# A causal attention and feed-forward block on one core: GELU by a tanh polynomial, half-tile streams, scores in batches of three, roots and squares on GpSimd

## What is computed

```python
def attention(x):                       # x: 4096 x 256
    q, k, v = split(lora_linear(x, w_attn, ...), 3)
    att = where(causal, q @ k.T / sqrt(16), -inf)
    return lora_linear(softmax(att) @ v, w_proj, ...)

def ffn(x):
    h = x
    for blk in range(3):
        y = qlora_linear(h, 2 * blk)
        y = layernorm(y, gamma[blk], beta[blk])
        y = gelu(y)                     # exact, with erf
        h = h + qlora_linear(y, 2 * blk + 1)
    return h

x = x + layernorm(attention(layernorm(x)))
x = x + layernorm(ffn(layernorm(x)))
```

## Time and profile before

| | |
|---|---|
| median of three runs | 1313.88 us |
| time of the profiled execution | 1311.47 us |
| its span, first to last instruction | 1309.7 us |
| granted TensorE clock, mean of the span | 0.990 |
| TensorE, VectorE, ScalarE, GpSimd busy in the span | 96%, 48%, 89%, 11% |
| stream, 119 to 1240 us: TensorE busy | 1105.92 of 1121 us |
| stream: ScalarE busy | 1073.11 of 1121 us |

### The profile page before, as it was taken

How to read it: one execution, slowest core, us unless ns; L and a number is a source line. 1 busy time by engine, 2 the same in 40 slices (tenths; PEclk the granted TensorE clock), 3 DMA queues, 4 the chain that set the end, 5 groups by cost and what they waited for, 6 DMA issues and landing times.

```text
span 1309.7 us, 30637 instructions
## 1 busy us (share of the span) xinstructions
PE 1257.4 (96%) x11725; PEld 534.9 (41%) x11725; DVE 629.6 (48%) x2202; ACT 1163.4 (89%) x1305; POOL 144.9 (11%) x347
## 2 busy tenths in 40 slices
PE   8998989999999999999999999999999999999956
PEld 6554434334333333333343333333333333333345
DVE  6774356334744266432743365433533355432176
ACT  4674879999999999999999999999999999999833
POOL 3321311010100000000000000000000010000043
PEclk9998989999999999999999999999999999999989
DMA  5994897786764366674754645445645474432000
GB/s 172 299 294 145 138 156 127 131 118 109 117 103 66 64 124 93 94 106 77 119 86 62 89 102 80 82 71 86 117 66 85 66 126 74 71 58 34 10 5 17
DMA packets 76498, 132.27 MB, mean 101 GB/s; under 512 B 21926, under 2 KB 37308, under 8 KB 76348
## 3 DMA queue, kind: packets, MB, share of 16 engines
q1 hardware_dynamic: 72060, 126.01, 54.5%
q10 hardware_dynamic: 4288, 4.26, 1.1%
HBM read 105.03 MB, written 20.97 MB: 96 GB/s over the span
## 4 chain that ended last, share of the span: by engine, by line
PE 74%; ACT 9%; issue 3%; DVE 2%; SPq 1%; DMA 1%; POOL 1%; ACTq 0%; DVEq 0%
PE O L1298 33%; PE S L1282 24%; PE F L205 14%; ACT probs L1224 6%; PE F L1344 2%; ACT L1224 1%; ACT L1240 1%; SPq L589 1%; ACT feed_mem L1240 1%; SPq L1129 1%; PE S L1363 1%; DMA attT<-o_div 1%; DVE tmpC L1403 0%; DMA q_op<-qk_rows 0%; DVE stC L1385 0%
## 5 line engine op out<-in xcount | busy, mean ns | idle before, releaser
L1224 ACT ACTIVATE probs<-S 128x1024 f32<-128x1024 f32 x1056 | 987.4, 1039 | 52.4 <-PE S L1282 42.1
L1298 PE MATMUL O<-probs,vg 128*32 128x512 f32 (+3 forms) x4608 | 528.6, 565 | 2.4 <-DVE o_turned L1437 1.7
L1282 PE MATMUL S<-q_op,k_op 64*128 64x512 f32 (+3 forms) x2304 | 391.5, 427 | 18.2 <-ACT probs L1224 6.5
L1282 PEld LDWEIGHTS S<-q_op,k_op 64*128 64x128 f32 x2304 | 181.9, 185 | 374.7 <-ACT probs L1224 305.3
L1205 POOL TENSOR_SCALAR_AFFINE_SELECT probs<-probs 128x512 f32<-128x512 f32 (+1 forms) x160 | 89.7, 561 | 1004.7 <-ACT probs L1224 1004.6
L1298 PEld LDWEIGHTS O<-probs,vg 128*32 128x32 f32 x4608 | 117.0, 109 | 202.1 <-issue 180.3
L1466 DVE TENSOR_TENSOR feed_mem<-F,bffn 128x512 f32<-128x512 f32 x56 | 38.7, 691 | 225.6 <-PE F L205 225.6
L205 PE MATMUL F<-wfT,feed_mem 128*32 128x256 f32 x1792 | 117.3, 384 | 0.9 <-ACT feed_mem L1240 0.9
L1472 DVE SCALAR_TENSOR_TENSOR feed_mem<-F,cols,feed_mem 128x256 f32<-128x256 f32 (+1 forms) x58 | 25.0, 473 | 138.7 <-PE F L205 138.7
L1469 DVE COPY feed_mem<-F 128x512 f32<-128x512 f32 x56 | 38.4, 686 | 81.1 <-PE F L1344 80.9
L1385 DVE BATCH_NORM_STATS2 stC<-feed_mem 128x6 f32<-128x256 f32 x172 | 64.7, 417 | 13.3 <-DVEq L1428 12.0
(11 more groups left out here) (165 smaller groups left out, 881.0 us busy)
## 6 DMA issues: line engine op xcount, KB each, us to landing
k_op<-qk_rows SPq DMA_DIRECT2D x512, 128.0 KB, 5.1
qk_rows<-parts SPq DMA_DIRECT2D x32, 512.0 KB, 4.8
q_op<-qk_rows SPq DMA_DIRECT2D x256, 64.0 KB, 5.8
k_op<-qk_rows SPq DMA_DIRECT2D x128, 64.0 KB, 2.9
x_in<-in_L_attn_x ACTq DMA_DIRECT2D x8, 512.0 KB, 5.5
feed_mem<-in_L_attn_x SPq DMA_DIRECT2D x16, 256.0 KB, 4.7
attT<-o_div SPq DMA_DIRECT2D x126, 32.0 KB, 3.6
out<-feed_mem SPq DMA_DIRECT2D x14, 256.0 KB, 2.6
```

The costliest lines, as they stand in the source:

```text
L1224: nc.scalar.activation(probs[:, n % NP, :, :], S[:, n % NS, :, :], ACT.Exp, scale=SCALE).then_inc(exp_ok, 1)
L1282: last = nc.tensor.matmul(S[:, n % NS, a, at:at + TT - q0], k_op[mine, c % RING, pair, k0:k0 + P], q_op[mine, v % QS, pair, q0:TT], start= ...
L1298: last = nc.tensor.matmul(O[h * STRIP:(h + 1) * STRIP, q0:TT], vg[:, kb, col:col + STRIP], probs[:, n % NP, a, at:at + TT - q0], start=fir ...
```

## The change

1. **GELU from tanh.** For tiles 0 to 6 the GELU is 0.5 v (1 + tanh(v p(v^2))), with a polynomial p of six degrees in the square. New parts of a half: `copy` now applies half of gamma and beta (two instructions of 128x256), `sq` squares (GpSimd), `pa`, `pb`, `pc` evaluate the polynomial (seven instructions on VectorE), ScalarE takes tanh (one instruction of 128x512 per half, in place of two for the tile) and `gate` multiplies (VectorE). Tile 7 keeps ScalarE's GELU.
2. **Roots on GpSimd.** The 84 roots of tiles 0 to 6 leave VectorE for GpSimd, as 11 instructions each.
3. **Half-tile streams.** The halves of a tile no longer follow a common order. Each keeps its own order of steps, and whichever is ready takes the bank `F`, which `plan()` locks until it is emptied. `FEED_EACH` falls from 70 to 50.
4. **Batches of three.** The planner lets three scores follow each other (`BATCH`), and weighs a switch of shape on TensorE against the time that ScalarE still has work for (`next_product`).
5. **Shared first keys.** Tiles 0 and 1 are visited in turn for each head group, from one chunk of two tiles of keys. There are 76 chunks instead of 80. Two key chunks and three query tiles are loaded early, instead of four and three. The ring of queries has four slots.

```diff
-RING, QS = 4, 3
+RING, QS = 4, 4
+EARLY_AT = {3: [("k", 0), ("q", 0)], 4: [("q", 1)], 5: [("k", 1)], 6: [("q", 2)]}
+VISITS = [(t, i) for i in range(NG) for t in range(2)] + [(t, i) for t in range(2, NT) for i in range(NG)]
...
-FEED_FROM, FEED_EACH = 24.0, 70.0
-LOW_WATER, FEED_WATER = 1, 3
+FEED_FROM, FEED_EACH = 24.0, 50.0
+BATCH, THIRD, SLACK, BACKLOG = 3, 0.25, 0.5, 10
+POOL_PARTS = ("rs", "sq")
+ROOT_POOL, SQUARE_POOL = 3.1, 1.3
...
+    if t < NT - 1 and name.startswith(POOL_PARTS):
+        return "POOL"
...
-    for m, x in enumerate(feed):
+    for x in feed:
         name, t, k, n = x
-        found = [feed[m - 1]] if m else []
+        if n:
+            found = [(name, t, k, n - 1)]
+        elif name != "project":
+            found = [(before, t, k, pieces(before, t) - 1)]
...
+    def next_product(now):
+        mine = ready["PE"]
+        score = next((x for x in mine if x[0] == "score"), None)
+        can = [x for x, at in mine.items() if at <= now and x[0] != "score"]
+        if score is not None and kind == "score" and batch < BATCH and mine[score] <= now + THIRD:
+            return score, max(now, mine[score])
...
+        def wish(x):
+            if x[0] == "weigh":
+                return 0.5 if backlog >= BACKLOG else 2
+            if due[x] <= scores / 2:
+                return 0 if kind == "feed" and x[3] else 1
+            return 4
...
+                    if t < NT - 1:
+                        a, c = tmp[:, 2, b], tmp[:, 3, b]
+                        nc.gpsimd.tensor_scalar(c, mv[:, b, 0], -1.0, None, ALU.mult)
+                        link(k, nc.gpsimd.tensor_tensor(w, r, r, ALU.mult))
+                        link(k, nc.gpsimd.tensor_tensor(w, w, v, ALU.mult))
...
+                        elif name.startswith("sq"):
+                            nc.gpsimd.tensor_tensor(u[:, rows(t, k), :], zT[:, :, toks(t, k)], zT[:, :, toks(t, k)], ALU.mult).then_inc(pool_ok[k], 1)
...
                         if t < NT - 1:
-                            for j in range(2):
-                                part_done(act, f"copy{m}", t, j)
+                            part_done(act, f"pc{m}", t, k)
+                            last = nc.scalar.activation(y[:, rows(t, k), :], y[:, rows(t, k), :], ACT.Tanh)
...
+                        if n == 5:
+                            link(k, nc.vector.tensor_scalar(y[:, b, :], u[:, b, :], GELU_POLY[6], None, ALU.mult))
+                        link(k, nc.vector.scalar_tensor_tensor(y[:, b, :], y[:, b, :], GELU_POLY[n], u[:, b, :], ALU.add, ALU.mult))
+                        nc.vector.scalar_tensor_tensor(y[:, b, :], y[:, b, :], GELU_POLY[n - 1], by, ALU.add, ALU.mult).then_inc(dve_ok[k], 1)
+                    elif name.startswith("gate"):
+                        nc.vector.scalar_tensor_tensor(zT[:, :, toks(t, k)], y[:, b, :], 1.0, zT[:, :, toks(t, k)], ALU.add, ALU.mult).then_inc(dve_ok[k], 1)
```

More of the change, by code:

```diff
@@ L965, in plan @@
             if t < NT - 1:
-                item((f"gelu{m}", t, 0), "ACT", 4.0, [(f"copy{m}", t, k) for k in range(2)], 0)
+                for k in range(2):
+                    item((f"gelu{m}", t, k), "ACT", 0.55, [(f"pc{m}", t, k)], 0)
             else:
@@ L992, in plan, with kind_of, shape_of, switch @@
             ready[engine[x]][x] = 0.0
-    scores, kind, shape = 0, None, None
+    scores, kind, shape, batch = 0, None, None, 0
+    def kind_of(x):
+        return x[0] if x[0] in ("score", "weigh") else "feed"
+    def shape_of(x):
+        return "score" if x[0] == "score" else "full" if x[0].startswith("turn") or len(x) == 4 and x[1] == NT - 1 else "strips"
+    def switch(x):
+        return 0.0 if shape_of(x) == shape else SWITCH[shape_of(x)]
+    def next_product(now):
[4 more added lines that the diff above has]
+            return score, max(now, mine[score])
+        busy = free["ACT"] + sum(us[x] for x, at in ready["ACT"].items() if at <= now + HOP)
+        first = score is not None and mine[score] <= now
+        slack = busy - (now + HOP + us[score] + SWITCH["score"]) if first else 1e9
+        pending = sum(1 for z in exp_ends[-8:] if z > now) + scores - len(exp_ends)
+        if first and pending >= NS - 1 and can:
+            slack = 1e9
+        weighed = (len([0 for x in can if x[0] == "weigh"]) and min(UNIT_OF[x[1]] for x in can if x[0] == "weigh"))
+        backlog = len(exp_ends) - weighed if weighed else 0
+        def wish(x):
[4 more added lines that the diff above has]
+            return 4
+        x = min(can, key=lambda x: (wish(x), -left.get(x, 0.0), mine[x], str(x)), default=None)
+        if first and (x is None or switch(x) + us[x] > slack + SLACK):
+            return score, now
+        return (x, now) if x is not None else (score, now)
     def landing(x):
         return LANDING_FIRST if x[0] == "moved" and x[1] < FIRST_MOVED else LANDING.get(x[0], 0.0)
+    locked, F_free, blocked = None, 0.0, {}
+    def takes_bank(x):
+        return len(x) == 4 and x[3] == 0 and (x[0] == "fold" or x[1] < NT - 1)
     exp_ends = []
```

166 lines of the change are left out of this document (106 added, 60 removed).

## The result

| | before | changed |
|---|---|---|
| median of the runs | 1313.6 us | 1305.7 us |
| smallest to largest | 1310.4 to 1315.1 us | 1303.2 to 1306.8 us |
| profiled execution, its span | 1311.5, 1309.7 us | 1305.5, 1303.7 us |
| first score to the end of the last exp, "the stream" | 1121.1 us | 1107.5 us |
| end of the last exp to the end, "the tail" | 69.6 us | 77.3 us |

The ratio is 0.9946, with an interval of 0.9935 to 0.9958, from six runs of each kernel. It is faster, by 8 us and not by the 46 forecast, and 1305.7 lies above the range. The last two rows of the table are read from the profiled executions. The stream gave 13.6 us where 48 were forecast, and the tail took 7.7 of them back where 2 were.

What follows compares the result with a forecast made beforehand. TensorE and ScalarE, both nearly full and tied by three score buffers, were taken as the bound. Terms -24 - 35 - 3 + 7 + 7 + 2 = -46 us took the profiled 1311.47 to 1265.5; predicted median 1268 us, range 1240 to 1303.

Steps and rivals of the forecast that it cites:

- Spells, -35: TensorE's order: 99 fewer rounds from scores to other work and back, at 0.35 us each, save 35 us.
- Table loads, -24: ScalarE: 42 table loads leave the stream; their 0.9% + 0.9% of the chain of waits is gained, 24 us.
- Third score +7: Score spells: a batch's third score waits for the running exp's buffer; at most 24 us, 7 taken.
- feed chain +7: Feed: late halves, with GpSimd and VectorE sharing ports, stop TensorE; 0 to 20 us, 7 taken.
- first keys -3: Loads: four fewer key chunks and a fourth query slot remove TensorE's query waits; 3 us saved (0 to 5).
- The sum of 409 us: GpSimd's busy time in the stream: cuts 90, roots 260 and squares 59 us, or 38%.
- Tail, +2 (0 to +7): After the last exp: tile 6's feed now ends at the stream's end, costing 2 us.
- C: Rival: the feed's chain leaks more and the third score costs 24 us; 1285 to 1308 us, chance 0.20.
- B: Rival: TensorE and ScalarE had waited for each other, so 20 us more go; 1236 to 1250 us, chance 0.13.
- D: Rival: slower, through GpSimd's roots held up by VectorE in each tile's chain; 1330 us, chance 0.12.
- the signs for being right: Two table loads, ScalarE about 1020 us, TensorE above 95%, stream about 1075 us, GpSimd near 410 us.
- The sign by which the forecast was to be called wrong: The stream stays over 1105 us though ScalarE's busy time fell by 50.

Runs made afterwards that it cites:

- c2: Kernel before, with every exp from the 13th on done over half of its columns: 1285.0 us.
- d4: Changed kernel without squares and polynomial, and with every exp from the 13th on over half of its columns: 1267.3 us.
- b1: Kernel before, with tanh in place of GELU in tiles 0 to 6 and the change's rule for TensorE's order: 1314.7 us.
- a1: Kernel before, with tanh in place of GELU in tiles 0 to 6, so that only the stream's 42 table loads go: 1298.1 us.
- b7: Changed kernel without squares and polynomial, tanh reading the turned tile directly: 1299.8 us.
- d3: b3 with visits, keys and query slots as in the kernel before: 1304.8 us.
- a3: Changed kernel with roots and squares of tiles 0 to 6 on VectorE, GpSimd keeping its cuts: 1314.3 us.
- b3: Changed kernel, but after the last score TensorE takes the last weighs ahead of tile 7's projection pieces: 1301.3 us.
- b4: Changed kernel with the planner's exp priced at the measured 0.935 us instead of 0.905: 1318.1 us.
- d2: b3 with the polynomial's parts and the copy priced in the plan at what the trace shows: 1315.1 us.
- e1: b3 with the polynomial at its measured price and weighs preferred from 11 unweighed exps on instead of 10: 1311.3 us.

## Why the prediction was wrong, step by step

The direction was right and every part was named. The error is in how the terms were added.

*Spells, -35: right in size, but not as time.* 99 fewer spells took 35.4 us off TensorE's own time (1089.1 to 1053.7), 0.36 each. c2 against d4, with ScalarE out of the way, give 37 for 94, and b1 against a1 23.1 for 79. The step that failed is what the forecast made of it: that TensorE "was busy throughout", so that its saving is the kernel's. b1 shows it alone: 23.1 us saved, 23.5 waited.

*Table loads, -24: measured -10 in the stream (a1), -14 by the medians.* I priced the loads by their share of the chain. A load that ends last is not worth its length; its removal is worth the distance to what ends second, here mostly TensorE's feed. The account of TensorE's waits could be drawn from the trace of before and is an upper bound, 32 us; 24 lies under it, so the bound alone would not have caught this term. I had used the right sentence, "in the rest of that time TensorE had weighs and feeds to do", and then let the chain decide how much that rest is.

*Third score +7, feed chain +7, first keys -3: together +11, measured +32.* That is the rise of TensorE's waits from a1's 21.6 to 53.8. For the third score I kept 24 as a bound and chose 7 "with ScalarE no longer full". By b1 the new rule costs 23.5 us of waits, and from a1 to the changed kernel the waits in spells of three alone rose by 25.6 (11.4 to 37.0). So the bound was what it cost. The likely reason, argued and not tested: ScalarE was not full, but there are three buffers and so no stock of scores, and a spell of three needs all of them. The feed chain is the smaller part. Tanh waited 5.8 us, and taking the polynomial away gave the stream 1.3 (b7). The first keys' 3 agree with d3 (3.5 between the medians).

*GpSimd.* A root is 12 instructions (lines 1267 to 1278) and not the 11 of the description and the sum. It took 3.2 us, where 3.1 were summed. First and last row of one on GpSimd:

```profile
206.19 0.23 POOL L1267 TENSOR_SCALAR tmpC<-mvC 128x2 f32<-128x2 f32 x1 [8.03 <-DVE rstdC L1488]
209.20 0.20 POOL L1278 TENSOR_TENSOR nmrC<-tmpC,rstdC 128x2 f32<-128x2 f32 x1
```

The sum of 409 us counted the pauses between a root's instructions as busy; the profile has 352. Squares took 1.11 us, not 1.4, and line 1512 waited 113 us for roots. None of this is seen on TensorE (0.8 us of waits for the feed's inputs), and with roots and squares on VectorE instead the kernel was slower (a3).

*Tail, +2 (0 to +7): measured +7.7.* I looked for tile 6's feed, and it was not that. Weighs stood behind tile 7's first pieces, which the order showed. b3 took back 4.4. Where the other 3 come from was not followed up.

New sum against before: -10.4 (tables), -35.4 (spells' own time), +32.2 (waits), +7.7 (tail) = -5.9 us, and the spans differ by 6.0. It closes by construction, since its terms are differences within the account; what the experiments add is which edit each belongs to.

*A reading.* The prediction put about 90% of the chain on TensorE and ScalarE; the page has 74% and 9%, so 83%. No term of the sum rests on it.

*Rivals.* The time is that of C (1285 to 1308, chance 0.20), whose second half, a third score at 24 us, is what happened; its first, the feed's leak, is not. B was excluded by the same coupling. D did not happen. Of the signs for being right, two table loads, ScalarE at 1019 us and TensorE at 97% of the stream came out, the stream near 1075 us and GpSimd near 410 did not. The sign by which the forecast was to be called wrong, a stream over 1105 us with ScalarE's busy time down by 50, came out: 1107.5 with 54 less.

**What stays open.** Why ScalarE and TensorE lose just this much to each other is not settled to a rule. TensorE's own time in the stream is 1054 us in the changed kernel, ScalarE is busy for 1019, and the stream is 1107. With ScalarE halved most of the waits go (5.7 us left in c2, 16.1 in d4). A fourth score buffer would test whether the three are the reason, and was not tried. The order is a search by rules of thumb: numbers closer to the trace made it worse three times (b4, d2, e1), so a few microseconds between two orders say little about the part that was edited.

## What to carry to other kernels

Where two engines with nearly equal work share few buffers, do not add savings on both: first sum, from the timeline, how long the bounding engine really waited for the other, and take that as the most that relieving the other can give (here 32 us, of which 10 came). A saving on the bounding engine counts only as far as the other can follow, so look at what its new rhythm asks of the buffers. A share of the chain of waits is no price, and after a gain in the stream look at the order at its end.
